# A recurrent layer and a gated feed-forward layer in one kernel: input projection by half blocks, two chains from the first state, VectorE pieces of one width, and five weight pieces rounded by GpSimd

## The chip, the cores and the metric

The kernel runs on 1 core of one Trainium2 chip. The time is device microseconds (us). Before the change the median of 3 runs is 580.43 us (580.22 to 582.93). The execution that the profile shows took 580.79 us, with a span of 579.0 us between its first and last instruction.

## The reference

For 2 sequences of 1024 tokens of 512 numbers, all in float32:

```python
# layer 1, recurrent
u = einsum('bsd,hd->bsh', layernorm(x), W_in) + b_in        # 512 -> 1024
s_t = tanh(u_t + s_{t-1} * gamma + beta)                     # 1024 steps, elementwise
x = x + layernorm(einsum('bsh,dh->bsd', s, W_out) + b_out)   # 1024 -> 512
# layer 2, feed-forward; q(w) rounds a weight to float8_e4m3fn and back
h = layernorm(x)
gate = silu((h @ q(gate_w)) * gate_scale)                    # 512 -> 1536
up = (h @ q(up_w)) * up_scale
x = x + layernorm(((gate * up) @ q(down_w)) * down_scale)    # 1536 -> 512
```

The recurrence is the only part that cannot be computed side by side: state t needs state t-1. The 36 weight pieces of layer 2 (128x512 each) are rounded once, during the first blocks.

## The kernel before

Time is cut into 8 blocks of 128 tokens, with both sequences in a block (256 rows). The names carry the block: u(n) is the input projection of block n, y(n,b) the output projection of its half b (64 tokens of both sequences), gate_up(p,i) and down(p,i) chunk i of 12 of layer 2 for block p.

The recurrence takes one step per token. A step is a scan on VectorE (preact = u + gamma * state, in PSUM) and a tanh on ScalarE that writes the state into `pairs`. The scan of the next step waits for that tanh. For states 0 to 255 one scan of 128x32 and one tanh carry both sequences (L1169, L1470: one chain). From state 256 on each sequence has a scan of 128x16 and a tanh of its own (L1160, L1466: two chains), and the second has the PSUM bank `recur_second`, which up to then served the rounding of weights.

All other work is laid between the steps by a planner. `Timetable.lay` goes through time in tenths of a step and gives each engine the able job of lowest rank; on VectorE and ScalarE a job takes one place between two steps. `timetable` states the jobs, what each waits for and its rank, with costs in steps (`U_STEPS` and the like, times `PACE`). TensorE's jobs run in the order in which they are stated; the table `BETWEEN` says before which chunk of block p a y, u or transpose stands ("y1" is y(p+1,1)). The planner gives places only. On the chip each engine runs its instructions in that order and waits at semaphores.

VectorE's work of a block comes in pieces: adding b_out to y (L1208), statistics (L1174), normalizing (L1227, L1263), the low part of x1 (L1279), scaling z (L1310), and the product of gate and up (L1297, "fused"). `row_parts` cuts most rows of blocks 2 to 7 into four pieces of 128 columns, where the first two blocks have two of 256; `chunk_parts` cuts the gate-up product of blocks 1 to 6 into two of 128 tokens.

A weight piece is rounded by adding and subtracting a constant per number (two VectorE instructions make the constant, L1345 and L1352). 24 pieces do it by three TensorE products into a PSUM bank and two ScalarE copies out of it (L1111 to L1113, L1517); 12 by two accumulating DMAs that GpSimd issues (L1603, L1614).

## Time and profile before

| | us |
|---|---|
| median of 3 runs | 580.43 |
| profiled execution, time | 580.79 |
| profiled execution, span | 579.0 |
| TensorE busy | 553.5 (96%) |
| VectorE busy | 447.2 (77%) |
| ScalarE busy | 371.6 (64%) |
| GpSimd busy | 204.5 (35%) |

The columns of a timeline row are the start, the duration, the engine, the line of the kernel and the shapes; at the end, in brackets, is the idle time of that engine just before and what ended it. Instructions of one engine overlap: the next one starts before the last has ended, so the distance between two starts is what an instruction costs its engine.

### The profile page before, as it was taken

What the parts mean: (1) busy time and instruction counts of PE and PEld (TensorE: products, weight loads), DVE (VectorE), ACT (ScalarE), POOL (GpSimd) and SP (SyncE); (2) the same over time, 40 slices, a digit from 0 to 9 for tenths busy, and PEclk for the clock granted to TensorE, in tenths of its full rate; (3) what the DMA queues carried; (4) which work ended last, traced back from release to release, by engine and by line L of the source; (5) the groups of instructions that cost most, each with busy time, mean ns of one, the idle gap of its engine ahead of it and who ended that gap; (6) DMA issues with size and microseconds to landing.
All of it is one profiled execution on the core that took longest, in us unless ns stands there. A gap on an engine that the chain in (4) does not pass through costs nothing.

```text
span 579.0 us, 11854 instructions
## 1 busy us (share of the span) xinstructions
PE 553.5 (96%) x2984; PEld 462.6 (80%) x2984; DVE 447.2 (77%) x2607; ACT 371.6 (64%) x2284; POOL 204.5 (35%) x339
## 2 busy tenths in 40 slices
PE   8999899899988999999999999999999999999993
PEld 5767667889776988788988799778986897889992
DVE  3689899996796888888988887789868988754313
ACT  3687687855686767866777677767776776523330
POOL 1214316435252323533334333152214341732622
PEclk9999999999998999999999999999999999999997
DMA  7878369800102001010102010020000200200000
GB/s 253 285 225 244 60 201 208 170 0 2 38 1 74 1 2 38 31 45 1 38 2 73 2 38 1 1 74 2 2 1 2 73 2 2 72 1 2 1 36 37
DMA packets 20069, 33.89 MB, mean 59 GB/s; under 512 B 2720, under 2 KB 4896, under 8 KB 20000
## 3 DMA queue, kind: packets, MB, share of 16 engines
q1 hardware_dynamic: 16544, 26.84, 13.8%
q0 software_dynamic: 3456, 6.29, 6.1%
q8 instruction: 24, 0.39, 0.3%
q14 instruction: 45, 0.37, 0.2%
HBM read 22.63 MB, written 4.19 MB: 46 GB/s over the span
## 4 chain that ended last, share of the span: by engine, by line
DVE 50%; ACT 24%; PE 17%; issue 5%; POOL 2%; SPq 0%; DMA 0%; POOLq 0%; DVEq 0%; ACTq 0%
DVE recur L1160 14%; ACT pairs L1466 10%; PE gate_up L1067 8%; DVE recur L1169 6%; DVE recur_second L1160 6%; DVE fused L1297 5%; ACT pairs L1450 4%; PE wide L1090 4%; ACT fused_hi L1509 3%; DVE peaks L1362 3%; ACT gated L1493 3%; PE wide L1026 3%; DVE powers L1345 2%; ACT pairs L1470 2%; DVE rounders L1352 2%
## 5 line engine op out<-in xcount | busy, mean ns | idle before, releaser
L1466 ACT ACTIVATE pairs<-recur 128x8 f32<-128x8 f32 x768 | 138.4, 180 | 100.2 <-DVE recur L1160 99.6
L1160 DVE TENSOR_TENSOR_SCAN recur<-recur,pairs 128x16 f32<-128x16 f32 x768 | 151.3, 197 | 56.0 <-ACT pairs L1466 51.8
L1592 POOL TENSOR_TENSOR fused_lo<-fused,fused_hi 128x256 fp32r<-128x256 f32 x96 | 71.1, 741 | 200.2 <-ACT fused_hi L1509 200.2
L1466 ACT ACTIVATE pairs<-recur_second 128x8 f32<-128x8 f32 x768 | 138.3, 180 | 0.0
L1160 DVE TENSOR_TENSOR_SCAN recur_second<-recur_second,pairs 128x16 f32<-128x16 f32 x768 | 133.4, 174 | 0.0
L1026 PE MATMUL wide<-w_out_sb,pairs 128*128 128x512 f32 x256 | 117.3, 608 | 5.7 <-ACT pairs L1466 5.7
L1067 PE MATMUL gate_up<-x_hi,gate_q 128*128 128x256 f32 x384 | 103.3, 302 | 3.5 <-DVE fused L1297 2.4
L1026 PEld LDWEIGHTS wide<-w_out_sb,pairs 128*128 128x128 f32 x256 | 74.4, 298 | 38.5 <-ACT pairs L1466 7.5
L1004 PE MATMUL wide<-x_norm_t,w_in_sb 128*128 128x256 f32 x448 | 101.0, 380 | 2.3 <-DVE y L1208 2.2
L1004 PEld LDWEIGHTS wide<-x_norm_t,w_in_sb 128*128 128x128 f32 x448 | 84.5, 190 | 16.0 <-issue 3.1
L1067 PE MATMUL gate_up<-x_lo,up_q 128*128 128x256 f32 x384 | 95.9, 283 | 0.0
L1067 PE MATMUL gate_up<-x_hi,up_q 128*128 128x256 f32 x384 | 95.7, 282 | 0.0
L1067 PE MATMUL gate_up<-x_lo,gate_q 128*128 128x256 f32 x384 | 95.2, 281 | 0.0
L1297 DVE SCALAR_TENSOR_TENSOR fused<-gate_up,up_scale_cols,gated 128x128 f32<-128x128 f32 (+1 forms) x168 | 57.9, 349 | 36.2 <-ACT gated L1493 36.2
L1067 PEld LDWEIGHTS gate_up<-x_hi,gate_q 128*128 128x128 f32 x384 | 72.1, 188 | 9.9 <-DVE fused L1297 3.5
L1090 PE MATMUL wide<-down_q,fused_hi 128*128 128x512 f32 x192 | 77.7, 405 | 0.0
L1067 PEld LDWEIGHTS gate_up<-x_lo,gate_q 128*128 128x128 f32 x384 | 72.4, 188 | 5.6 <-issue 3.1
L1090 PE MATMUL wide<-down_q,fused_lo 128*128 128x512 f32 x192 | 75.8, 395 | 0.0
L1067 PEld LDWEIGHTS gate_up<-x_lo,up_q 128*128 128x128 f32 x384 | 72.4, 189 | 0.0
L1067 PEld LDWEIGHTS gate_up<-x_hi,up_q 128*128 128x128 f32 x384 | 72.3, 188 | 0.0
L1169 DVE TENSOR_TENSOR_SCAN recur<-recur,pairs 128x32 f32<-128x32 f32 x256 | 58.9, 230 | 17.0 <-ACT pairs L1470 13.4
L1470 ACT ACTIVATE pairs<-recur 128x16 f32<-128x16 f32 x256 | 48.2, 188 | 36.8 <-DVE recur L1169 34.0
(126 smaller groups left out, 763.8 us busy)
## 6 DMA issues: line engine op xcount, KB each, us to landing
x_in<-x SPq DMA_DIRECT2D x16, 256.0 KB, 3.3
x_res<-x SPq DMA_DIRECT2D x16, 256.0 KB, 3.2
out<-z SPq DMA_DIRECT2D x14, 256.0 KB, 2.5
w_in_sb<-w_in_t SPq DMA_DIRECT2D x4, 512.0 KB, 6.1
w_out_sb<-w_out_t SPq DMA_DIRECT2D x8, 256.0 KB, 4.3
raw_own<-down_w SPq DMA_DIRECT2D x8, 256.0 KB, 3.8
raw_own<-rounders POOLq DMA_DIRECT2D x6, 256.0 KB, 4.5
raw_own<-gate_w SPq DMA_DIRECT2D x5, 256.0 KB, 4.1
```

The source lines that it names most:

```text
L1004: ins = eng.matmul(wide[bank][:, jj * TOK:(jj + 1) * TOK], w_in_sb[:, k, j * P:(j + 1) * P], x_norm_t[:, k, :], start=(k == 0), stop=(k == ...
L1026: ins = eng.matmul(wide[b][:, :], pairs_by_batch[:, state_slots(n, b), :, j, 0].rearrange("p s b -> p (s b)"), w_out_sb[:, j, :], start=(j ...
L1067: ins = eng.matmul(gate_up[g][:, v, :], w_q[:, k, i * P:(i + 1) * P], part[:, k, :], start=(k == 0 and part is x1_hi), stop=(k == KD - 1 a ...
L1090: ins = eng.matmul(wide[2 + b][:, :], part[:, f, b * P:(b + 1) * P], down_q[:, i, :], start=(i == 0 and part is fused_hi), stop=(i == KI - ...
L1160: eng.tensor_tensor_scan(preact_of[b].rearrange("p c k -> p (c k)"), factors_of[b].rearrange("p c k -> p (c k)"), pairs[:, (t - 1) % RING, ...
L1169: eng.tensor_tensor_scan(preact.rearrange("p c k -> p (c k)"), factors.rearrange("p c k -> p (c k)"), pairs[:, (t - 1) % RING, :, :].rearr ...
L1297: eng.scalar_tensor_tensor(out=fused[:, f, ts], in0=gate_up[i % NG][:, 1, ts], scalar=up_scale_cols[:, i:i + 1], in1=gated[:, f, ts], op0= ...
L1362: eng.tensor_reduce(peaks[:, i, h:h + 1], pieces[i][1][:, halves(h)].bitcast(F32), AX_X, ALU.max, apply_absolute_value=True).then_inc(s_pe ...
L1450: ins = eng.activation(pairs_by_batch[:, slots, :, j, 1].rearrange("p s b -> p (s b)"), wide[m % 2][:, at_bank:at_bank + count * batch], A ...
L1466: eng.activation(pairs[:, t % RING, columns, 0], preact_of[b][:, :, 1], ACT.Tanh).then_inc(s_state_of[b], 1)
L1470: eng.activation(pairs[:, t % RING, :, 0], preact[:, :, 1], ACT.Tanh).then_inc(s_state, 1)
L1592: eng.tensor_tensor(fused_lo[:, f, :], fused[:, f, :], fused_hi[:, f, :].bitcast(F32), ALU.subtract).then_inc(s_fused_lo, 1)
```

## The change

- Both chains run from the first state, each sequence with a PSUM bank of its own (`recur0`, `recur1`). `recur_second` goes; the tensor rounding alternates between two banks instead of three.
- All row pieces are halves of 256 columns, and a gate-up product is one piece of 256 tokens in every block.
- The input projection is made by half blocks: 128 columns of one half instead of 256 of both, 16 products an item as against 8. A half can be projected and copied without the other. Block 2's first half is laid ahead of state 128.
- Weight pieces 7, 11, 15, 19 and 23 are rounded on GpSimd by an add and a subtract of 128x512 ("lift", "drop"). 19 pieces stay on TensorE and ScalarE, 12 on DMAs.
- The planner's tables move with it; looking for the weights' peaks starts at step 120 instead of 60. In TensorE's order the last y, y(7,1), stands two chunks later.

```diff
 BETWEEN = {
...
-    6: {4: "y1", 12: "t0 t1"},
+    6: {1: "y02", 2: "y03", 6: "y1", 12: "t0 t1"},
 }
-PEAKS_FROM = 60.0
+PEAKS_FROM = 120.0
+POOL_PIECES = (7, 11, 15, 19, 23)
+ADD_STEPS, LIFT_RANK = 2.7, 0.0
-TWO_CHAINS_FROM = 2
-def row_parts(kind, n, b, last):
-    if kind == "x":
-        return 4 if n >= TWO_CHAINS_FROM + 2 else 2
-    if kind in ("z", "low"):
-        return 2
-    return 2 if n < 2 or (n, b) == (last, 1) else 4
-def chunk_parts(p, last):
-    return 2 if 1 <= p < last else 1
...
-        recur = ps("recur", [P, 2, CH, 2])
-        preact = recur[:, 0, :, :]
-        factors = recur[:, 1, :, :]
+        recur = [ps(f"recur{b}", [P, 2, KH, 2]) for b in range(batch)]
+        preact = [recur[b][:, 0, :, :] for b in range(batch)]
+        factors = [recur[b][:, 1, :, :] for b in range(batch)]
-        recur_second = ps("recur_second", [P, 512])
-        round_banks = [recur_second[:, :], wide[2][:, :], wide[3][:, :]]
+        round_banks = [wide[2 + b][:, :] for b in range(batch)]
...
             def project_u():
-                        for jj in range(2):
-                            j = 2 * m + jj
+                        for jj in range(4):
+                            j = 4 * bank + jj
                             for k in range(KD):
-                                ins = eng.matmul(wide[bank][:, jj * TOK:(jj + 1) * TOK],
-                                                 w_in_sb[:, k, j * P:(j + 1) * P], x_norm_t[:, k, :],
+                                ins = eng.matmul(wide[bank][:, jj * P:(jj + 1) * P],
+                                                 w_in_sb[:, k, j * P:(j + 1) * P], x_norm_t[:, k, g * P:(g + 1) * P],
                                                  start=(k == 0), stop=(k == KD - 1))
...
             def recurrence():
-                    if t >= SPLIT:
-                        for b in range(batch):
...
-                    eng.tensor_tensor_scan(preact.rearrange("p c k -> p (c k)"), factors.rearrange("p c k -> p (c k)"),
-                                           pairs[:, (t - 1) % RING, :, :].rearrange("p c k -> p (c k)"), 0.0,
-                                           ALU.mult, ALU.add).then_inc(s_preact, 1)
+                    for b in range(batch):
+                        if t == 0:
+                            eng.wait_ge(s_bias, 1 + batch)
+                        else:
+                            eng.wait_ge(s_state[b], t)
+                        eng.tensor_tensor_scan(preact[b].rearrange("p c k -> p (c k)"),
+                                               factors[b].rearrange("p c k -> p (c k)"),
+                                               pairs[:, (t - 1) % RING, b * KH:(b + 1) * KH, :].rearrange(
+                                                   "p c k -> p (c k)"), 0.0, ALU.mult, ALU.add).then_inc(s_preact[b], 1)
...
             def fuse():
-                        for h in token_pieces(p):
-                            ts = token_slice(p, h)
-                            eng.scalar_tensor_tensor(out=fused[:, f, ts], in0=gate_up[i % NG][:, 1, ts],
-                                                     scalar=up_scale_cols[:, i:i + 1], in1=gated[:, f, ts],
-                                                     op0=ALU.mult, op1=ALU.mult).then_inc(s_fused, 1)
+                        eng.scalar_tensor_tensor(out=fused[:, f, :], in0=gate_up[i % NG][:, 1, :],
+                                                 scalar=up_scale_cols[:, i:i + 1], in1=gated[:, f, :],
+                                                 op0=ALU.mult, op1=ALU.mult).then_inc(s_fused, 1)
...
+            def round_pieces():
+                for i in range(NP):
+                    if not by_pool(i):
+                        continue
+                    yield at["lift", i]
+                    eng.wait_ge(s_raw_in[raw_of[i]], 16 * (raw_use[i] + 1))
+                    eng.wait_ge(s_constant, i + 1)
+                    eng.tensor_tensor(raw[raw_of[i]], raw[raw_of[i]], rounders[rounder_of[i]].bitcast(F32),
+                                      ALU.add).then_inc(s_lifted, 1)
+                    yield at["drop", i]
+                    eng.wait_ge(s_lifted, pool_pieces(i + 1))
+                    eng.tensor_tensor(pieces[i][1], raw[raw_of[i]], rounders[rounder_of[i]].bitcast(F32),
+                                      ALU.subtract).then_inc(s_dropped, 1)
```

What stands on VectorE between the scans of steps 0 to 1023, counted over the instructions in order (1023 places, at most one instruction in each):

| between two steps | before | after |
|---|---|---|
| nothing | 313 | 497 |
| an aggregate or another of a few columns | 61 | 59 |
| a piece of 128 columns | 240 | 0 |
| a piece of 256 columns | 200 | 320 |
| a gate-up product of 128 tokens | 126 | 0 |
| a gate-up product of 256 tokens | 12 | 76 |
| 128x512, for a weight's constant | 71 | 71 |

In TensorE's order, 61.5 us of work stand between the starts of y(6,1) and y(7,1) after the change, 57.7 us before, and 483.8 us ahead of y(7,1), 484.7 us before (the counts of products times the durations that the trace shows for their kinds).

VectorE in block 3, where y(3,0) is taken up. Before (an instruction named `recur` or `recur_second` is a scan):

```order
L1160 SCALAR_TENSOR_TENSOR recur_second<-recur_second,pairs 128x16
L1208 TENSOR_TENSOR y<-wide,b_out_rows 128x128
L1160 SCALAR_TENSOR_TENSOR recur<-recur,pairs 128x16
L1160 SCALAR_TENSOR_TENSOR recur_second<-recur_second,pairs 128x16
L1208 TENSOR_TENSOR y<-wide,b_out_rows 128x128
L1160 SCALAR_TENSOR_TENSOR recur<-recur,pairs 128x16
L1160 SCALAR_TENSOR_TENSOR recur_second<-recur_second,pairs 128x16
L1208 TENSOR_TENSOR y<-wide,b_out_rows 128x128
```

After the change:

```order
L1234 SCALAR_TENSOR_TENSOR fused<-gate_up,up_scale_cols,gated 128x256
L1110 SCALAR_TENSOR_TENSOR recur<-recur,pairs 128x16 x2
L1151 TENSOR_TENSOR y<-wide,b_out_rows 128x256
L1110 SCALAR_TENSOR_TENSOR recur<-recur,pairs 128x16 x2
L1151 TENSOR_TENSOR y<-wide,b_out_rows 128x256
L1110 SCALAR_TENSOR_TENSOR recur<-recur,pairs 128x16 x2
```

Four places with a piece of 128 columns have become two with 256, and the gate-up product ahead of them is one of 256.

TensorE around the first output projection (`w_out_sb`), in the time of rounding. Before:

```order
L1004 MATMUL wide<-x_norm_t,w_in_sb 128x256 x8
L1026 MATMUL wide<-w_out_sb,pairs 128x512 x8
L1004 MATMUL wide<-x_norm_t,w_in_sb 128x256 x16
L1111 MATMUL wide<-x_norm,ident 128x512
L1112 MATMUL wide<-x_lo,fused_hi 128x512
```

After the change:

```order
L1072 MATMUL wide<-rounders,fused_hi 128x512
L1073 MATMUL wide<-rounders,fused_hi 128x512
L986 MATMUL wide<-w_out_sb,pairs 128x512 x8
L1071 MATMUL wide<-x_res,ident 128x512
L1072 MATMUL wide<-rounders,fused_hi 128x512
L1073 MATMUL wide<-rounders,fused_hi 128x512
L961 MATMUL wide<-x_norm_t,w_in_sb 128x128 x32
```

The input projections are twice as many products of half the columns, and half of block 1's stand ahead of the y.

GpSimd in the same time, after the change (`L1558` is the lift, `L1562` the drop; the DMA rows are issues for the other pieces):

```order
L1558 TENSOR_TENSOR x_res<-x_res,rounders 128x512
L1548 DMA up_q<-z 128x512
L1481 TENSOR_SCALAR norms<-mean_var_y 128x1
L1484 TENSOR_TENSOR norms<-norms,minus_half 128x1
L1548 DMA up_q<-x_norm 128x512
L1512 TENSOR_TENSOR x_res<-y,x_res 128x512
L1562 TENSOR_TENSOR up_q<-x_res,rounders 128x512
L1558 TENSOR_TENSOR raw_own<-raw_own,rounders 128x512
```

The roots of the norms (`norms`) and the residual add (`L1512`), which VectorE waits for, now stand among lifts and drops.

## Rows read from the trace of the kernel before

**Rows 1.** The page: the busy time of each engine.

```profile
PE 553.5 (96%) x2984; PEld 462.6 (80%) x2984; DVE 447.2 (77%) x2607; ACT 371.6 (64%) x2284; POOL 204.5 (35%) x339
```

**Rows 2.** Timeline of TensorE: first and last of four y that waited for a state.

```profile
175.30 5.04 PE L1026 MATMUL wide<-w_out_sb,pairs 128*128 128x512 f32 x7 [3.87 <-ACT pairs L1466]
...
442.89 1.63 PE L1026 MATMUL wide<-w_out_sb,pairs 128*128 128x512 f32 x3 [0.81 <-ACT pairs L1466]
```

**Rows 3.** Timeline of VectorE: the first and the last scan.

```profile
17.75 0.23 DVE L1169 TENSOR_TENSOR_SCAN recur<-recur,pairs 128x32 f32<-128x32 f32 x1 [3.37 <-ACT pairs L1431]
...
501.15 0.20 DVE L1160 TENSOR_TENSOR_SCAN recur<-recur,pairs 128x16 f32<-128x16 f32 x1
```

**Rows 4.** The chain of waits after the last state: start, duration, what.

```profile
501.77 7.18 PE wide L1026 x16
508.95 1.91 PE gate_up L1067 x16
510.86 0.93 PE wide L1090 x4
...
568.84 0.76 DVE z L1310 x2
```

**Rows 5.** Timeline of VectorE, two chains: steps with nothing between.

```profile
300.33 0.20 DVE L1160 TENSOR_TENSOR_SCAN recur<-recur,pairs 128x16 f32<-128x16 f32 x1 [0.16 <-ACT pairs L1466]
...
300.78 0.20 DVE L1160 TENSOR_TENSOR_SCAN recur<-recur,pairs 128x16 f32<-128x16 f32 x1 [0.16 <-ACT pairs L1466]
```

**Rows 6.** The same, a step with a piece of 128 columns.

```profile
313.42 0.20 DVE L1160 TENSOR_TENSOR_SCAN recur<-recur,pairs 128x16 f32<-128x16 f32 x1
...
313.62 0.27 DVE L1208 TENSOR_TENSOR y<-wide,b_out_rows 128x128 f32<-128x128 f32 x1
313.87 0.20 DVE L1160 TENSOR_TENSOR_SCAN recur<-recur,pairs 128x16 f32<-128x16 f32 x1
```

**Rows 7.** The same, a step with a piece of 256 columns.

```profile
302.25 0.18 DVE L1160 TENSOR_TENSOR_SCAN recur<-recur,pairs 128x16 f32<-128x16 f32 x1
...
302.43 0.41 DVE L1310 TENSOR_TENSOR z<-wide,down_scale_rows 128x256 f32<-128x256 f32 x1
302.75 0.18 DVE L1160 TENSOR_TENSOR_SCAN recur<-recur,pairs 128x16 f32<-128x16 f32 x1
```

**Rows 8.** The same, the one step with a gate-up product of 256 tokens.

```profile
146.48 0.20 DVE L1160 TENSOR_TENSOR_SCAN recur<-recur,pairs 128x16 f32<-128x16 f32 x1 [0.22 <-ACT pairs L1466]
...
146.67 0.46 DVE L1297 SCALAR_TENSOR_TENSOR fused<-gate_up,up_scale_cols,gated 128x256 f32<-128x256 f32 x1
147.05 0.19 DVE L1160 TENSOR_TENSOR_SCAN recur<-recur,pairs 128x16 f32<-128x16 f32 x1
```

**Rows 9.** Timeline of VectorE, one chain: a step with an instruction of 128x512.

```profile
89.05 0.23 DVE L1169 TENSOR_TENSOR_SCAN recur<-recur,pairs 128x32 f32<-128x32 f32 x1
89.19 0.41 DVE L1345 TENSOR_SCALAR powers<-raw_own 128x512 int32<-128x512 int32 x1
89.53 0.23 DVE L1169 TENSOR_TENSOR_SCAN recur<-recur,pairs 128x32 f32<-128x32 f32 x1
```

**Rows 10.** The chain of waits: input projections of 128 and of 256 columns.

```profile
9.49 7.16 PE wide L968 x64
...
61.05 7.14 PE wide L1004 x32
```

**Rows 11.** Timeline of TensorE: the starts of two rounded pieces.

```profile
21.37 1.02 PE L1111 MATMUL wide<-raw_own,ident 128*128 128x512 f32 x2
...
22.69 1.02 PE L1111 MATMUL wide<-raw_own,ident 128*128 128x512 f32 x2
```

**Rows 12.** GpSimd's adds of 128x512, and one instruction each of GpSimd and VectorE.

```profile
L1578 POOL TENSOR_TENSOR x_res<-y,x_res 128x512 f32<-128x512 f32 x15 | 19.5, 1303 | 9.7 <-DVE y L1227 9.7
...
134.67 0.78 POOL L1560 TENSOR_SCALAR x_in<-x_in,norms 128x512 f32<-128x512 f32 x1
...
134.81 0.78 DVE L1263 TENSOR_SCALAR x_norm<-x_res,mean_var_r,norms 128x256 f32<-128x256 f32 x1
```

More of the change, by code:

```diff
@@ L128, in lay @@
                 steps = job.steps
-                if engine not in ("vector", "scalar") and self.two_chains_from <= now < self.last_step:
+                if engine not in ("vector", "scalar") and 0 <= now < self.last_step:
                     steps *= PACE
@@ L245, in project_u @@
     def project_u(n, m, k):
-            after = [((*("t1_copy", n, b), h), 0.2) for b in range(batch) for h in range(2)]
+            g = m // 2
+            after = [(v, 0.2) for v in pair("t1_copy", n, g)]
             if m >= 2:
@@ L444, in lay_first @@
             if i == 2:
-                after += converted(i for i in range(NP) if not by_transfer(i))
+                after += converted(i for i in range(NP) if by_tensor(i))
             if i == FIRST_Y_AT_CHUNK:
@@ L490, in timetable @@
                 if i < KI:
-                    low = [(v, 0.2) for b in range(batch) for v in rows("low", "x1_low", p, b)] if i == 0 else []
+                    low = [(v, 0.2) for b in range(batch) for v in pair("x1_low", p, b)] if i == 0 else []
                     gate_up(p, i, low, rank(n - 1, 4.5) + 0.01 * i)
@@ L508, in timetable @@
         norm_z(LAST, b, ("down", LAST, KI - 1), rank(NB, 10 + b))
-    last_piece = max(i for i in range(NP) if not by_transfer(i))
-    for h in range(2):
-        side("vector", ("second", h), [(v, 0.2) for v in pair("take", last_piece)], 90.0)
     t.jobs["down", 0, KI - 1].after.append((("guard", 3), 0.2))
```

379 lines of the change are left out of this document (170 added, 209 removed), and 10 rows, old and new, of the table BETWEEN.

## The prediction, made before the changed kernel ran

> **What bounds the kernel now.** I read the page's busy times first, then TensorE's timeline for its waits, then the chain of waits behind the last state, then VectorE's timeline step by step. TensorE is busy for 553.5 us, 96% of the span [rows 1], which looks like the bound. But its timeline shows output projections that waited for a state: y(2,0) for 3.87 us and, the last of four, y(6,1) for 0.81 us [rows 2]. The last scan starts at 501.15 [rows 3] and y(7,1) at 501.77 [rows 4]: TensorE gets there as its state gets ready. Behind it the chain is TensorE alone up to 568.84, and then the norm and store of the last rows until the span's end at 579.0 [rows 4]. So the end is the start of y(7,1) plus what is left for TensorE (67.1 us) plus 10.2 us, and that start is the later of two things: the recurrence (1023 steps in 483.4 us, 0.473 each [rows 3]) and TensorE's own work ahead of it.
>
> What a step costs is set by VectorE. With two chains a step with nothing between takes 0.45 us, from scan to scan [rows 5]; there VectorE idles and the tanh is waited for. A piece of 128 columns fits into that idle time: 0.45 [rows 6]. A piece of 256 columns doesn't: 0.50 [rows 7]. A gate-up product of 256 tokens makes it 0.57 [rows 8]. With one chain a step with an instruction of 128x512 takes 0.48 [rows 9].
>
> **The change part by part.** *Wider pieces.* Quarters become halves in blocks 2 to 7 and two gate-up products become one. By the counts of the 1023 places between steps: 1023 x 0.45 = 460.4; 320 pieces of 256 columns at 0.05 more, 16.0; 76 wide gate-up products at 0.12 more, 9.1; 71 instructions of 128x512. The trace has none of these last between two chains. From below they cost as a piece of 256 columns (0.05), since their 0.41 us is that piece's [rows 7, 9]; from above as a gate-up product (0.12). I take 0.07, near the first: 5.0. Pieces of a few columns cost nothing. Together 490.5.
>
> The same prices for the kernel before (200 pieces of 256, 12 wide products, 71 at 0.05) give 460.4 + 10.0 + 1.4 + 3.6 = 475.4, where 483.4 were measured [rows 3]. The other 8.0 are waits, two input copies in one step, and the first 255 steps, which had one chain. I carry them over.
>
> *Two chains from the first state.* In the first 255 steps one chain cost 0.48 with a wide instruction between [rows 9], two chains cost 0.50, so about 200 filled places lose 0.02 each, 4.0, and about 50 empty ones gain up to 0.03, 1.5. The bounds of the sum are -1.5 (the filled ones lose nothing) and +4.0 (the empty ones gain nothing); I take 1.5, between them, since both kinds are in the order.
>
> The recurrence then ends at 17.75 + 490.5 + 8.0 + 1.5 = 517.8, against 501.15, and y(7,1) can start 0.6 later, as before: 518.4.
>
> *TensorE.* Five rounded pieces go. One costs 1.32 us, from start to start [rows 11]: 6.6 us less. The half-block input projections double the instructions, but 64 of 128 columns take 7.16 us and 32 of 256 take 7.14 [rows 10], so they cost 0. With two rounding banks instead of three a rounding product can wait for a copy two pieces back; that falls into the time ahead of y(2,0), where TensorE had 3.87 us to wait [rows 2], and I take 0. Ahead of y(7,1) are 483.8 us of work, 0.9 less than before, because that y stands two chunks later (2 x (1.91 + 0.93) = 5.7 [rows 4]). With the idle time of before (501.77 - 484.7 = 17.1) TensorE would be there at 500.9. It won't be: y(6,1) waits for state 896, and from there 61.5 us of TensorE's work stand against 128 steps of about 0.48, also 61.5. So TensorE and state arrive together again, near 518, and I take the state's 518.4; if TensorE is behind, by 1 to 2 us.
>
> *Behind y(7,1)* are 67.1 - 5.7 = 61.4 us [rows 4]. The six chunks behind the last y give 17 us for its norms (6 x 2.84); before there were eight, 22.7.
>
> *Lifts and drops.* Ten adds of 128x512 on GpSimd, 1.30 us each by the nearest row [rows 12]: 13 us on an engine that is busy 35% of the time [rows 1]. They take 10 of ScalarE's copies away, which lay between steps and cost nothing. What they can cost is VectorE's time: while GpSimd worked on 134.67 to 135.45, a VectorE instruction of 256 columns ran for 0.78 [rows 12], where such a piece else takes 0.41 [rows 7], with the next scan queued behind it. The least is 0, the most 10 x 1.30 = 13 us. I take 0, because the 15 such adds of before [rows 12] can have cost only a part of the 8.0 us that all waits made; the range keeps the rest. DMA issues that queue behind a lift on GpSimd come up to 1.3 us later, for weights that are used far later. Of this the Trainium skill (SBUF — State Buffer, Who interferes with whom) says that the two engines share a port pair as an exclusive lock, and whichever comes second blocks for the whole instruction. The row agrees with it, 0.78 against 0.41 us; taken at its worst for all ten, it gives the 13 us of the second rival.
>
> *Sum.* 518.4 + 61.4 + 10.2 = 590.0 of span; with the 1.8 us around it (580.79 - 579.0) 591.8; the median of the runs was 0.4 below the profiled time, so 591.5, which is 1.9% slower.
>
> **Rivals.** *The wider pieces relieve the recurrence: faster.* VectorE would save instructions (240 quarters and 126 halves become 120 and 64), the steps would run at the empty step's pace, and TensorE's saving would come out: y(7,1) at 500.9, the end at 500.9 + 61.4 + 10.2 + 1.8 = 574.3. It decides if steps average below 0.46. For it: 366 short instructions become 184. Against it: the short pieces cost nothing in their steps [rows 6], so there is nothing to save, and the wide ones stand out [rows 7, 8]. The Trainium skill (VectorE: DVE Perf Modes, The TRN2 errata) would have it this way: a fixed latency per instruction, so that few wide tiles beat many small ones. The steps of this trace don't bear it out: 0.57 for a wide product, 0.45 for a step that holds a short piece.
>
> *The lifts collide: slower still.* If six of the ten hold up a VectorE instruction for 1.3 us each, and the scan behind it, the end is some 8 us later: 600. For it: the lock in rows 12, and that 71 instructions of weights stand in the same stretch. Against it: the planner keeps such pairs apart, and few collided before.
>
> *The saving makes up for it: no change.* If only half of the added 17 us comes, because steps with an empty place behind a wide one catch up, the recurrence ends at 509 and the end is near 583; at 507 it is the time of before. The rows speak against it: after a wide step the next one is not shorter than 0.45 [rows 5, 6].
>
> **How the numbers follow.** Forecast 0.77 (its own range 587 to 597), collision 0.10, faster 0.06, no change 0.07. The predicted time is the forecast's, 591.5. The range 585 to 600 takes in the uncertain terms: 4 us below for carried waits that may shrink, 3 below for the 128x512 and one-chain terms; 8 above for collisions and a late TensorE. A measurement tells about 0.5% (2.9 us) from no change. Faster 0.06; within 0.5% 0.06 (the case of no change but for its slower end); slower 0.88.
>
> **What would show it.** Right: the last scan starts near 518, steps with a 256-column piece take 0.50 and with a product 0.57; y(2,1) to y(7,1) mostly wait for a state, longer than before; from y(7,1)'s start to the last product 61 us; TensorE's busy time near 547. Wrong: the last scan before 510 (the prices of wide pieces fail), VectorE instructions of weights that last over 0.8 us beside a lift (collision), a gap on TensorE ahead of the last x1 transposes (the 17 us were too few), TensorE late at y(2,0) for want of a rounding bank, or input products of 128 columns at more than 0.115 us each.

## The result, and the profile after

The changed kernel takes 594.66 us (median of 4 runs, 593.08 to 596.07), the kernel before 580.35 (4 runs beside them). The ratio of their means is 1.0235, with a 95% interval of 1.0196 to 1.0274. By the medians it is slower by 14.3 us. The forecast was 591.5 us in a range of 585 to 600. The profiled execution of the changed kernel took 594.35 us, its span 592.6.

First the page of the changed kernel, the busy time of each engine.

```profile
PE 554.9 (94%) x3412; PEld 477.5 (81%) x3412; DVE 434.6 (73%) x2664; ACT 379.4 (64%) x2530; POOL 218.5 (37%) x349
```

Against [rows 1], VectorE has 12.6 us less to do and GpSimd 14.0 more. TensorE, which gave five rounded pieces away, is not less busy but 1.4 us more: 554.9, where the prediction had 547.

The timeline of VectorE in the changed kernel, the first and the last scan (start, duration, what):

```profile
18.06 0.28 DVE L1110 TENSOR_TENSOR_SCAN recur<-recur,pairs 128x16 f32<-128x16 f32 x2 [4.06 <-ACT pairs L1369]
...
517.19 0.28 DVE L1110 TENSOR_TENSOR_SCAN recur<-recur,pairs 128x16 f32<-128x16 f32 x2 [0.16 <-ACT pairs L1403]
```

The chain of waits of the changed kernel from the last state on, and further down in it the first row of z:

```profile
518.48 1.90 PE gate_up L1027 x16
521.31 6.87 PE wide L986 x16
528.18 1.91 PE gate_up L1027 x16
...
579.11 3.27 PE wide L1050 x14
...
582.40 0.76 DVE z L1246 x2
```

Against [rows 3] the last scan is 16.0 us later (517.19 for 501.15). Against [rows 4], y(7,1) starts 19.5 us later, and from there to z are 61.1 us instead of 67.1. So the 13.6 us that the span grew are 16.0 of recurrence, plus 3.5 because TensorE came to y(7,1) later than the state (521.31 - 517.19 is 4.1 us, before it was 0.6), minus 6.0 behind it.

The 16.0 us of recurrence can be split at step 256, ahead of which no piece on VectorE became wider. The scan of that step on VectorE's timeline, in the kernel before and in the changed one:

```profile
145.48 0.20 DVE L1160 TENSOR_TENSOR_SCAN recur<-recur,pairs 128x16 f32<-128x16 f32 x1 [0.47 <-ACT pairs L1470]
```

```profile
151.71 0.27 DVE L1110 TENSOR_TENSOR_SCAN recur<-recur,pairs 128x16 f32<-128x16 f32 x2
```

From the first scan to this one took 127.7 us before and 133.7 after, 5.9 more; from this one to the last 355.7 and 365.5, 9.8 more; 0.3 lie ahead of the first scan.

The steps of the changed kernel, on VectorE's timeline with two chains: empty ones and, at 301.48, one with a wide gate-up product.

```profile
300.08 0.28 DVE L1110 TENSOR_TENSOR_SCAN recur<-recur,pairs 128x16 f32<-128x16 f32 x2 [0.17 <-ACT pairs L1403]
300.53 0.28 DVE L1110 TENSOR_TENSOR_SCAN recur<-recur,pairs 128x16 f32<-128x16 f32 x2 [0.17 <-ACT pairs L1403]
300.97 0.28 DVE L1110 TENSOR_TENSOR_SCAN recur<-recur,pairs 128x16 f32<-128x16 f32 x2 [0.16 <-ACT pairs L1403]
301.48 0.28 DVE L1110 TENSOR_TENSOR_SCAN recur<-recur,pairs 128x16 f32<-128x16 f32 x2 [0.23 <-ACT pairs L1403]
301.67 0.46 DVE L1234 SCALAR_TENSOR_TENSOR fused<-gate_up,up_scale_cols,gated 128x256 f32<-128x256 f32 x1
302.05 0.27 DVE L1110 TENSOR_TENSOR_SCAN recur<-recur,pairs 128x16 f32<-128x16 f32 x2
```

0.45 and 0.44 empty (the third empty one took 0.51), 0.57 with the product (301.48 to 302.05): the prices of [rows 5] and [rows 8] hold here. Over all steps from state 256 on, the changed kernel has 449 empty ones of 0.456 us on average, 206 with a piece of 256 columns of 0.498 and 67 with a wide product of 0.569. In the kernel before, 240 steps with a piece of 128 columns took 0.461 and 126 with a product of 128 tokens 0.445. What the prediction priced at 0 lies in the first two blocks. VectorE's and then GpSimd's timeline there:

```profile
74.33 0.28 DVE L1110 TENSOR_TENSOR_SCAN recur<-recur,pairs 128x16 f32<-128x16 f32 x2
74.51 1.98 DVE L1281 TENSOR_SCALAR powers<-z 128x512 int32<-128x512 int32 x1
76.41 0.27 DVE L1110 TENSOR_TENSOR_SCAN recur<-recur,pairs 128x16 f32<-128x16 f32 x2
```

```profile
74.00 0.89 POOL L1537 DMA_DIRECT2D z<-rounders  x1 [2.55 <-DVE rounders L1288]
74.65 1.54 POOL L1562 TENSOR_TENSOR up_q<-raw_own,rounders 128x512 fp32r<-128x512 f32 x1
```

An instruction of weights that takes 0.41 us by itself [rows 9] lasted 1.98 beside a DMA issue and a drop, and ended 0.3 us behind the drop; the step took 2.08 us. The 71 steps with an instruction of 128x512 average 0.619 in the changed kernel, with a median of 0.52: 7.1 us over the median, nearly all of it in eight steps, five of them beside a lift or a drop (5.1 us). In three of these five the lift or drop had begun first, as here, on VectorE's and then GpSimd's timeline:

```profile
80.79 1.23 DVE L1281 TENSOR_SCALAR powers<-raw_own 128x512 int32<-128x512 int32 x1
```

```profile
80.16 1.56 POOL L1562 TENSOR_TENSOR up_q<-x_res,x_lo 128x512 fp32r<-128x512 f32 x1
```

VectorE's instruction ended at 82.02, again 0.3 us behind the drop. And TensorE waits in this stretch. Its timeline, four of the waits:

```profile
60.74 9.01 PE L961 MATMUL wide<-x_norm_t,w_in_sb 128*128 128x128 f32 x64 [2.43 <-DVE y L1151]
...
77.06 1.12 PE L1071 MATMUL wide<-z,ident 128*128 128x512 f32 x2 [2.19 <-DVE x_lo L1288]
...
106.85 0.63 PE L1005 MATMUL wide<-ident,x_norm 128*128 128x128 f32 x4 [2.01 <-ACT down_q L1451]
...
114.84 0.39 PE L1027 MATMUL gate_up<-x_hi,gate_q 128*128 128x256 f32 x1 [3.35 <-DVE x_lo L1219]
```

The first 150 us in one row each (length, then busy time of PE, PEld, DVE, ACT, POOL, granted clock, DMA), of the kernel before and of the changed kernel:

```profile
0.00:150.00 150.00, 142.01 (x679) 108.67 (x680) 121.00 (x513) 99.84 (x455) 51.23 (x84) 1.00 0.59 159
```

```profile
0.00:150.00 150.00, 132.45 (x737) 105.10 (x738) 125.42 (x730) 103.31 (x668) 58.67 (x82) 0.97 0.60 159
```

TensorE was idle for 8.0 us before and for 17.6 after. Up to the start of y(7,1) it was busy for 486.0 us before and 493.4 after, and idle for 15.8 and 27.9. So two things in the result were open. The total came out 3 us from the forecast although the lifts did collide and TensorE was late: did the terms cancel? And what made TensorE late, when its work should have shrunk?

### The profile page after: what moved, and what is told of

The parts are those of the page before. It is cut to its first block, busy times and chain, and to the rows that moved or that the text cites. A ratio compares the mean times of both kernels' runs of the same rounds, so it can differ in the third digit from the quotient of the medians.

```text
span 592.6 us, 13054 instructions
## 1 busy us (share of the span) xinstructions
PE 554.9 (94%) x3412; PEld 477.5 (81%) x3412; DVE 434.6 (73%) x2664; ACT 379.4 (64%) x2530; POOL 218.5 (37%) x349
## 3 DMA queue, kind: packets, MB, share of 16 engines
q1 hardware_dynamic: 16544, 26.84, 13.6%
q0 software_dynamic: 3456, 6.29, 6.1%
## 4 chain that ended last, share of the span: by engine, by line
DVE 41%; ACT 29%; PE 24%; issue 4%; DMA 1%; POOL 1%; SPq 0%; POOLq 0%; DVEq 0%; ACTq 0%
DVE recur L1110 21%; ACT pairs L1403 14%; PE gate_up L1027 11%; ACT pairs L1389 6%; PE wide L1050 5%; PE wide L986 5%; DVE fused L1234 4%; ACT gated L1427 3%; DVE peaks L1298 3%; ACT fused_hi L1443 2%; PE wide L961 2%; DVE powers L1281 2%; DVE y L1151 1%; DVE x_norm L1204 1%; DVE x_lo L1219 1%
## 5 line engine op out<-in xcount | busy, mean ns | idle before, releaser
L1403 ACT ACTIVATE pairs<-recur 128x8 f32<-128x8 f32 x2048 | 264.3, 180 | 144.6 <-DVE recur L1110 144.1
L1110 DVE TENSOR_TENSOR_SCAN recur<-recur,pairs 128x16 f32<-128x16 f32 x2048 | 280.8, 183 | 98.5 <-ACT pairs L1403 89.7
L1027 PE MATMUL gate_up<-x_hi,gate_q 128*128 128x256 f32 x384 | 105.3, 307 | 11.0 <-DVE x_lo L1219 9.1
L961 PEld LDWEIGHTS wide<-x_norm_t,w_in_sb 128*128 128x128 f32 x896 | 106.4, 196 | 7.9 <-ACT x_norm_t L1356 3.5
L961 PE MATMUL wide<-x_norm_t,w_in_sb 128*128 128x128 f32 x896 | 107.6, 280 | 4.5 <-DVE y L1151 2.4
L1234 DVE SCALAR_TENSOR_TENSOR fused<-gate_up,up_scale_cols,gated 128x256 f32<-128x256 f32 x96 | 44.6, 464 | 33.4 <-ACT gated L1427 33.2
L1427 ACT ACTIVATE gated<-gate_up,gate_scale_cols 128x256 f32<-128x256 f32 x96 | 45.2, 470 | 32.6 <-PE gate_up L1027 32.6
L1389 ACT ACTIVATE pairs<-wide,u_bias 128x128 f32<-128x128 f32 (+2 forms) x136 | 54.2, 446 | 1.6 <-PE wide L961 1.6
L1443 ACT CAST fused_hi<-fused 128x256 fp32r<-128x256 f32 x96 | 38.4, 400 | 10.8 <-DVE fused L1234 10.5
L1050 PEld LDWEIGHTS wide<-down_q,fused_lo 128*128 128x128 f32 x192 | 36.1, 188 | 5.2 <-issue 0.5
```

The source lines that it names most:

```text
L961: ins = eng.matmul(wide[bank][:, jj * P:(jj + 1) * P], w_in_sb[:, k, j * P:(j + 1) * P], x_norm_t[:, k, g * P:(g + 1) * P], start=(k == 0) ...
L1027: ins = eng.matmul(gate_up[g][:, v, :], w_q[:, k, i * P:(i + 1) * P], part[:, k, :], start=(k == 0 and part is x1_hi), stop=(k == KD - 1 a ...
L1050: ins = eng.matmul(wide[2 + b][:, :], part[:, f, b * P:(b + 1) * P], down_q[:, i, :], start=(i == 0 and part is fused_hi), stop=(i == KI - ...
L1110: eng.tensor_tensor_scan(preact[b].rearrange("p c k -> p (c k)"), factors[b].rearrange("p c k -> p (c k)"), pairs[:, (t - 1) % RING, b * K ...
L1234: eng.scalar_tensor_tensor(out=fused[:, f, :], in0=gate_up[i % NG][:, 1, :], scalar=up_scale_cols[:, i:i + 1], in1=gated[:, f, :], op0=ALU ...
L1389: ins = eng.activation(pairs_by_batch[:, slots, :, j, 1].rearrange("p s b -> p (s b)"), wide[bank][:, at_bank:at_bank + count * batch], AC ...
```

## The experiments

The theory: the recurrence sets the end, and its length is the width of VectorE's pieces. The rivals: it is the lifts; or it is TensorE. I undid parts in the changed kernel, and made parts alone in the kernel before. The ratio compares each with the kernel before on the same chip (there 580.5 to 582.3 us). The time is the median of 4 to 12 executions; the last scan and y(7,1) are read from one profiled execution, which can be off that median by 2.5 us: it took 597.2 us with wide pieces and 601.0 with y(7,1) earlier, the longest of four each, and 595.88 without lifts, the shortest of four.

| kernel | last scan | y(7,1) starts | time, us | ratio to before, interval |
|---|---|---|---|---|
| before | 501.15 | 501.77 | 580.35 | |
| changed | 517.19 | 521.31 | 594.66 | 1.0235 (1.0196 to 1.0274) |
| before, wide pieces | 517.56 | 518.15 | 594.71 | 1.023 (1.02 to 1.026) |
| changed, narrow pieces | 509.02 | 515.28 | 588.22 | 1.0111 (1.0086 to 1.0136) |
| changed, no lifts | 512.37 | 522.83 | 597.77 | 1.0268 (1.024 to 1.0295) |
| changed, both undone | 505.48 | 517.62 | 590.98 | 1.0152 (1.0135 to 1.0169) |
| before, lifts | 515.06 | 515.68 | 594.85 | 1.0235 (1.0212 to 1.0257) |
| before, y(7,1) later | 502.29 | 508.60 | 582.41 | 1.0007 (0.9992 to 1.0022) |
| before, lifts and y(7,1) later | 515.24 | 521.57 | 595.42 | 1.0246 (1.0221 to 1.0272) |
| before, two chains from the start | 503.87 | 507.22 | 586.48 | 1.0087 (1.0062 to 1.0111) |
| before, two rounding banks | 500.80 | 501.45 | 581.80 | 1.0015 (0.9998 to 1.0031) |
| before, split input products | 502.70 | 503.35 | 583.86 | 1.0037 (1.0023 to 1.005) |
| changed, y(7,1) earlier | 519.67 | 520.26 | 598.59 | 1.0307 (1.0281 to 1.0334) |
| before, z and low in quarters | 498.10 | 507.80 | 586.57 | 1.0096 (1.0079 to 1.0113) |

**The wide pieces alone, on the kernel before.**

```
 def row_parts(kind, n, b, last):
-    if kind == "x":
-        return 4 if n >= TWO_CHAINS_FROM + 2 else 2
 ...
+    return 2
 def chunk_parts(p, last):
-    return 2 if 1 <= p < last else 1
+    return 1
```

> The kernel before with VectorE's side work in wide pieces only (halves of 256 columns for every y, x, residual and z, the gate-up product over 256 tokens at once); two chains, input products, rounding and order as before. Theory A (the price of a recurrence step follows the width of the piece that stands in it): 120 more steps with a 256-column piece at 0.05 us and 64 more with the wide product at 0.12 us, 13.7 us, so the last scan near 515 us instead of 501.15 and a time of 591 to 595 us. Rival B (the later end comes from GpSimd's lifts and drops and from the new order, not from width): last scan within 3 us of 501, time 578 to 583 us. Rival C (wide pieces relieve VectorE, fewer instructions): last scan before 501, time under 579 us.

Last scan 517.56, time 594.71: theory A, and the two rivals that deny the width are out, on this kernel. The last scan moved by 16.4 us, for 13.7 expected; but the profiled execution was 2.5 us longer than the median. There are long steps in the trace, which no price of a piece explains. One of them, on VectorE's timeline:

```profile
503.05 0.20 DVE L1156 TENSOR_TENSOR_SCAN recur<-recur,pairs 128x16 f32<-128x16 f32 x1 [0.16 <-ACT pairs L1462]
...
505.15 0.42 DVE L1306 TENSOR_TENSOR z<-wide,down_scale_rows 128x256 f32<-128x256 f32 x1 [1.81 <-PE wide L1086]
505.49 0.19 DVE L1156 TENSOR_TENSOR_SCAN recur<-recur,pairs 128x16 f32<-128x16 f32 x1
```

The step took 2.44 us: a piece of z stands in VectorE's order ahead of the next scan and waits for TensorE, which the longer recurrence has put behind its plan. From state 256 on four steps took 1.5 to 2.4 us each, three of them with a piece of y or z that waited so; the fourth (1.82) stands in the kernel before too (1.81). These three are 4.1 us over a usual step, a step ahead of them took 3.25 us where it took 1.56 before, and the first scan came 0.4 us later. That leaves some 10 us for the width.

**The narrow pieces put back into the changed kernel** (quarters, and the gate-up product in two halves, planner and waits with them).

```
+def row_parts(kind, n, b, last):
+    if kind == "x":
+        return 4 if n >= TWO_CHAINS_FROM + 2 else 2
 ...
+def chunk_parts(p, last):
+    return 2 if 1 <= p < last else 1
```

> The changed kernel with the narrow pieces of the kernel before put back (quarters of y, x and residual in the later blocks, the gate-up product in two halves of 128 tokens in blocks 1 to 6); two chains from the start, half-block input products, five pieces on GpSimd and the new order stay. Theory A: the last scan falls by 12 to 14 us, to 503 to 505 us; y(7,1) then starts when TensorE comes to it, between 503 and 510 us, and with 61 us behind it the time is 575 to 583 us. Rival B (lifts, drops and order made the later end): last scan stays at 514 to 517 us, time 590 to 595 us. Rival T (TensorE sets the end, with its dearer input products and its lower clock): last scan earlier, but y(7,1) not before 515 us, time 588 us or more.

8.2 us of the last scan come back, not 12 to 14, and 6 to 7 of the time (588.22 for 594.66; ratio 1.0111 for 1.0235). The last scan on VectorE's timeline, and y(7,1) in the chain of waits:

```profile
509.02 0.28 DVE L1162 TENSOR_TENSOR_SCAN recur<-recur,pairs 128x16 f32<-128x16 f32 x2
```

```profile
515.28 6.87 PE wide L1038 x16
```

The numbers are rival T's: the last scan is earlier, but y(7,1) starts at 515.28, 6 us behind the state, and the time is 588.22. That the width lengthens the recurrence holds as well, all of it behind step 256 (365.5 us from there on with wide pieces, 357.1 with narrow ones). And TensorE's arrival hangs on the width too. Its waits for the low part of x1 (line, engine waited for, us in total, times, longest) from 150 to 515 us, in the changed kernel and then with narrow pieces:

```profile
PE gate_up L1027 <- DVE x_lo L1219: 5.7, 3, 2.5
PE wide L986 <- DVE x_lo L1219: 1.7, 1, 1.7
```

```profile
PE gate_up L1079 <- DVE x_lo L1273: 2.4, 3, 1.1
```

7.4 us became 2.4, which is most of the 6.0 us by which y(7,1) starts earlier (515.28 for 521.31); in the kernel before it was 1.0. VectorE makes x1's low part between its steps, so what makes the steps longer can reach TensorE this way.

**No lifts in the changed kernel.**

```
-POOL_PIECES = (7, 11, 15, 19, 23)
+POOL_PIECES = ()
```

> The changed kernel with no piece of weights rounded by GpSimd (24 pieces on TensorE in the two banks); the rest as changed. In the profile of the changed kernel nine steps of the first two blocks that meet a lift or a drop are 7 us over the median together. Theory A with collisions as a second cause: these steps go back to 0.5 us, last scan at 509 to 512 us instead of 517; TensorE has five pieces of 1.32 us more, 6.6 us, ahead of y(7,1), which then starts at 515 to 522 us; time 588 to 595 us. Rival without collisions (the long steps have another source, transfers of weights or ScalarE): last scan stays at 516 to 518 us, time 594 to 599 us. Rival B (collisions and order are all of it): last scan near 503 us.

The last scan is at 512.37, 4.8 us earlier, as theory A has it but for 0.4 us, and the 71 steps of 128x512 average 0.517 instead of 0.619. The collisions were the lifts'. These steps alone give back 7.2 us; others became longer, one of 2.76 us with a copy of y. But y(7,1) starts at 522.83, 10.5 us behind the state, and the time of 597.77 is above theory A's range: with five pieces more TensorE alone sets the end. The lifts cost the recurrence 4.8 us, and taking them out doesn't make this kernel faster; the intervals of the two ratios overlap.

**Half-block products alone, on the kernel before.** Each product of 256 columns as two of 128.

```
-for jj in range(2):
-    j = 2 * m + jj
+for jj in range(4):
+    j, g = 2 * m + jj // 2, jj % 2
     for k in range(KD):
-        eng.matmul(wide[bank][:, jj * TOK:(jj + 1) * TOK], ..., x_norm_t[:, k, :], ...)
+        eng.matmul(wide[bank][:, jj * P:(jj + 1) * P], ..., x_norm_t[:, k, g * P:(g + 1) * P], ...)
```

> The kernel before with each input product of 256 columns (28 items of 8 products, blocks 1 to 7) done as two products of 128 columns into the same bank; copies, order and the rest unchanged. Theory H (the half-width products cost 0.2 us more per item, as 3.49 us against 3.26 us in the two profiles): 28 items make TensorE 5 to 7 us busier, 559 us instead of 553.5, and since TensorE hardly waits in this kernel the time is 583 to 587 us. Rival K (the 3.49 us are a lower clock in that stretch, or waits inside an item, and the products cost the same per column): TensorE 553 to 555 us busy, time 579.5 to 582 us.

Between the theories, and nearer to H: TensorE is 3.1 us busier (556.6), half of what H said, and the time of 583.86 is in H's range, 0.37% or some 2.2 us over the kernel before beside it. The line of these products, in the kernel before, in this one and in the changed kernel (busy us, mean ns, idle before). Each product of the program leaves two instructions in the trace, so an item of 8 products of 256 columns shows as x16 and one of 16 of 128 as x32.

```profile
L1004 PE MATMUL wide<-x_norm_t,w_in_sb 128*128 128x256 f32 x448 | 101.0, 380 | 2.3 <-DVE y L1208 2.2
```

```profile
L1004 PE MATMUL wide<-x_norm_t,w_in_sb 128*128 128x128 f32 x896 | 104.3, 275 | 2.2 <-DVE y L1208 2.0
```

```profile
L961 PE MATMUL wide<-x_norm_t,w_in_sb 128*128 128x128 f32 x896 | 107.6, 280 | 4.5 <-DVE y L1151 2.4 <-ACT x_norm_t L1356 2.0
```

The split costs this line 3.3 us, half of the 6.6 that rounding saves. In the chain of waits one item shows it: 16 instructions of 256 columns (from the kernel with y(7,1) later, below, which has them whole), and 32 of 128 (from the one with both losses undone):

```profile
284.08 3.45 PE wide L1004 x16
```

```profile
292.13 3.57 PE wide L1013 x32
```

28 items at 0.12 us more are 3.4 us. The changed kernel's line has another 3.3 us. A part of it comes with a lower granted clock: the 64 instructions behind the wait of 2.43 us at 60.74 took 9.01 us, where 64 such take 7.16 [rows 10], and the mean granted clock from 60 to 70 us was 0.83.

**The lifts alone, on the kernel before** (the same five pieces, with `round_pieces` of the changed kernel).

> The kernel before with pieces 7, 11, 15, 19 and 23 rounded by GpSimd (lift and drop) instead of TensorE; narrow pieces, chains, input products and order as before. Theory A (lifts and drops hold up VectorE's instructions of weights, and the scan behind them): TensorE 6.6 us less busy, near 547, but the last scan 3 to 7 us later, 504 to 508 us, and the time 583 to 587 us. Rival S (no collision of weight, and the state sets y(7,1) anyway): last scan 500 to 502, time 579.5 to 581.5 us, the saving idle. Rival N (TensorE alone is the bound): time 573 to 577 us.

The mechanism of theory A, but two to four times its size: the last scan is 13.9 us later and the time 594.85. TensorE is not near 547 us either but busy for 553.0, at a granted clock of 0.973 over the whole run (0.991 in the kernel before). VectorE's and ScalarE's timelines at the longest step:

```profile
68.45 0.23 DVE L1206 TENSOR_TENSOR_SCAN recur<-recur,pairs 128x32 f32<-128x32 f32 x1
68.59 0.41 DVE L1389 TENSOR_SCALAR rounders<-powers 128x512 fp32r<-128x512 f32 x1
74.74 0.23 DVE L1206 TENSOR_TENSOR_SCAN recur<-recur,pairs 128x32 f32<-128x32 f32 x1 [5.74 <-ACT pairs L1507]
```

```profile
74.22 0.48 ACT L1487 ACTIVATE pairs<-wide,u_bias 128x128 f32<-128x128 f32 x1 [5.80 <-PE wide L1041]
74.50 0.21 ACT L1507 ACTIVATE pairs<-recur 128x16 f32<-128x16 f32 x1
```

A step of 6.29 us. Ten other steps with an instruction of weights were over 0.62 us, up to 2.28. By step 85 the recurrence was 7.1 us behind that of the kernel before (67.00 for 59.88). VectorE's copy of y came late with it, and TensorE's input projection waited 7.19 us for it (to 67.69, where [rows 10] has it start at 61.05); ScalarE's copy of that projection stands ahead of a tanh; and the scan waits for the tanh. The profile of the changed kernel has eight such steps and none over 2.08 us, and at step 85 it is 1.6 us behind (61.48): no such chain of waits formed there. Which part of its new order prevents it was not tried.

**y(7,1) two chunks later, alone and with the lifts, on the kernel before.**

```
-    6: {4: "y1", 12: "t0 t1"},
+    6: {6: "y1", 12: "t0 t1"},
```

> The kernel before with the last output projection, y(7,1), two chunks later in TensorE's order (at chunk 6 of block 6 instead of 4), nothing else. Theory A (state and TensorE come together at y(7,1)): the two chunks, 5.7 us, go ahead of it, TensorE comes to it at 506 to 508 us, and the time stays at 579 to 582 us. Rival S (TensorE could have come earlier and the state alone sets it): y(7,1) at 502 to 503, time 574 to 577 us.

> Both of the former together: the kernel before with five pieces rounded by GpSimd and y(7,1) two chunks later. Theory A (TensorE and the recurrence each bound the start of y(7,1), so only lighter TensorE work ahead of it and the later place together pay): TensorE at y(7,1) near 501.8 + 5.7 - 6.6 = 501 us, the state there at 502 to 508 depending on collisions, 61.4 us behind it, time 575 to 582 us. Rival (collisions cost what is saved): last scan 507 us or later, time 581 us or more.

Alone: no change (1.0007), y(7,1) at 508.60, as theory A has it but for 0.6 us: what no longer stands behind y(7,1) stands ahead of it. With the lifts: 595.42, the rival, since the last scan is at 515.24 as with the lifts alone.

**Two chains from the start, and two banks alone, on the kernel before.** The first: `TWO_CHAINS_FROM = 0`, the second chain's bank taken out of `round_banks`, its factors filled at the head. The second leaves the chains:

```
-round_banks = [recur_second[:, :], wide[2][:, :], wide[3][:, :]]
+round_banks = [wide[2][:, :], wide[3][:, :]]
```

> The kernel before with two chains from the first state and therefore two banks for rounding instead of three; narrow pieces, 24 pieces on TensorE, full input products and order as before. Theory A (as forecast for this edit): last scan 1.5 us later (0 to 4), 501 to 505 us, time 580 to 584 us, TensorE's idle time ahead of 150 us within 2 us of the 8 us of before. Rival B (two banks and wide weight instructions between two chains hold TensorE and the weights up early): TensorE idle 4 us or more longer ahead of 150 us, last scan 505 us or later, time 585 us or more.

> The kernel before with two banks for rounding (those of the down products) instead of three; one chain up to state 256 and two behind, 24 pieces on TensorE, order as before. Theory A (as the prediction took it: the bank costs nothing, what two chains from the start cost lies in the chains): time 579.5 to 582 us, TensorE's idle time ahead of 150 us 8 to 10 us as before. Rival B (the missing bank makes rounding products wait for copies, and the weights, x1 and the input products behind them): idle time ahead of 150 us 12 us or more, time 584 to 587 us, as with two chains from the start.

The banks are free (1.0015, the interval holds 1). The chains are not. They cost the recurrence 2.7 us, inside the forecast for that edit and theory A's range, but the time 5.1 (0.87%), since TensorE falls behind: its idle time and the time are rival B's, and not for the banks that B named. The first 150 us with two chains from the start, and with two banks alone:

```profile
0.00:150.00 150.00, 134.40 (x620) 101.22 (x621) 123.66 (x754) 108.70 (x693) 48.72 (x80) 0.98 0.61 159
```

```profile
0.00:150.00 150.00, 140.78 (x673) 107.30 (x674) 120.10 (x505) 98.31 (x447) 51.24 (x83) 0.99 0.60 159
```

15.6 and 9.2 us of TensorE idle; before it was 8.0, in the changed kernel 17.6. ScalarE is 8.9 us busier than before with two chains. The longest wait of TensorE in that stretch, in the kernel with two chains from the start:

```profile
113.17 1.22 PE L1001 MATMUL wide<-x_norm_t,w_in_sb 128*128 128x256 f32 x2 [5.39 <-ACT pairs L1441]
```

It waited for ScalarE's input copies. That the second chain's tanhs made these late is what the busier ScalarE suggests; it was not tried apart.

**Both losses of the recurrence undone in the changed kernel** (narrow pieces and no lifts).

> The changed kernel with two parts undone at once: narrow pieces as before and no piece rounded by GpSimd (24 pieces on TensorE in two banks). What is left of the change: two chains from the start with two banks, half-block input products, the new order. Theory A (the recurrence's losses add: 8.2 us for the width and 4.8 us for the lifts, by undoing one at a time): last scan at 503 to 505 us, as in the kernel before with two chains from the start; TensorE, with 5 pieces of 1.32 us more than with lifts, sets y(7,1), at 513 to 520 us, and the time is 586 to 593 us. Rival B (the two losses lie in one another, the state waits for TensorE): last scan at 507 us or later. Rival C (with both gone the state sets the end again): y(7,1) within 1 us of the last state, time under 580 us.

The last scan is at 505.48, just past theory A's range. Seen from this kernel, the width costs 6.9 us (512.37 - 505.48), the lifts 3.5 (509.02 - 505.48), and both 11.7 (517.19). They nearly add. One early step of 4.24 us in this trace, with a copy of y (2.76 without lifts alone), makes the first two look smaller: from step 256 on, where the widths differ, the wide pieces cost 9.0 us (365.7 for 356.7). The 590.98 are TensorE's, 12.1 us behind the state at y(7,1). Against the kernel without lifts y(7,1) is 5.2 us earlier (517.62 for 522.83): TensorE's waits for the low part of x1 from 150 us on fell from 7.4 to 2.4 us here too.

**y(7,1) earlier in the changed kernel** (chunk 4 instead of 6 of block 6).

> The changed kernel with y(7,1) back at chunk 4 of block 6, two chunks earlier; nothing else. Theory A (state 1024 at 517.8 us sets its start, TensorE was 3.5 us late): y(7,1) starts at 518 to 519 us with 66.8 us behind it instead of 61.1, time 596 to 598 us. Rival T (TensorE's work alone sets the end, the place of y(7,1) doesn't matter): time 593.5 to 595 us.

y(7,1) starts with its state, at 520.26, and the time is 598.59, just over theory A's range. The recurrence was 2.5 us longer in the profiled execution, for steps of the first two blocks; that execution took 601.0 us. The row of y(7,1) on TensorE's timeline, and the stretch behind it:

```profile
520.26 8.91 PE L986 MATMUL wide<-w_out_sb,pairs 128*128 128x512 f32 x16 [2.11 <-ACT pairs L1403]
```

```profile
520.00:530.00 10.00, 9.74 (x25) 5.98 (x26) 3.06 (x10) 0.46 (x3) 2.70 (x4) 0.83 0.01 2
```

After the wait the product took 8.91 us instead of 6.87, at a granted clock of 0.83. In the changed kernel, where TensorE came late and didn't wait, the same product took 6.87.

**A version meant to beat both:** the kernel before with z and the low part of x1 in quarters too.

```
     if kind in ("z", "low"):
-        return 2
+        return 4 if (kind == "z" or n > 0) and n < last else 2
```

> The kernel before with the pieces that were still 256 columns wide beside the recurrence narrowed too: z (copy and statistics) of blocks 0 to 6 and the low part of x1 of blocks 1 to 6 in quarters of 128 columns, about 80 pieces. Theory A (steps pay for width, 80 x 0.05 = 4 us, but TensorE becomes the bound, since of its waits for states only 0.59 and 0.81 us lie late): last scan at 497 to 499 us, y(7,1) at 500 to 501 us, time 577.5 to 580 us. Rival S (the state alone sets the end): time 575.5 to 577.5 us. Rival R (more instructions cost VectorE more than width): last scan 501 us or later, time 580.5 us or more.

The last scan is at 498.10, 3.1 us earlier: the price by width holds this way too. The time is 586.57, slower, which none of the theories had. TensorE's and GpSimd's timelines ahead of y(7,1):

```profile
505.73 0.80 PE L1090 MATMUL wide<-down_q,fused_hi 128*128 128x512 f32 x1 [2.47 <-POOL fused_lo L1592]
```

```profile
502.49 2.50 POOL L1584 TENSOR_TENSOR z<-z,x_res 128x512 f32<-128x512 f32 x2
504.95 2.10 POOL L1592 TENSOR_TENSOR fused_lo<-fused,fused_hi 128x256 fp32r<-128x256 f32 x3
```

With more pieces in VectorE's queue the last statistics of z come so late (GpSimd takes them up at 498.61, before at 493.41) that GpSimd does block 6's z just then, and the low part of a gate-up product, which TensorE needs, stands behind it. Another 2.6 us of TensorE's waits behind 150 us are for normalized rows of VectorE, which cost it none in the kernel before. y(7,1) starts at 507.80, 9.7 us behind the state. None of these versions beats the kernel before.

## Why the prediction was right

*The end is the later of the state's and TensorE's arrival at y(7,1), plus 61 us, plus 10.* Right, and 61.1 us were measured for 61.4. The last scan came at 517.19 for 517.8.

*Wider pieces, 15.1 us (490.5 - 475.4).* Right in kind, too dear in size. 13.7 of it lie behind step 256 (120 pieces at 0.05, 64 products at 0.12); undone in the changed kernel they were 8.4 and 9.0 us there, made alone on the kernel before some 10 without its waits, and 9.8 is what the changed kernel lost there. A piece of 256 columns costs its step 0.04 over an empty one (0.498 against 0.456) and not 0.05. And the steps of before were not all at 0.45: its 275 empty ones behind step 256 average 0.464, waits that the prediction carried over whole among its 8.0 us.

*Two chains from the first state, 1.5 us.* 2.7 us of recurrence, inside the bounds. What the step left out is TensorE: 7.6 us of idle time in the first 150 us.

*Lifts and drops, 0.* This step failed. They cost the recurrence 3.5 to 4.8 us, inside the bound of 13. The rival spoke of a planner that keeps such pairs apart. It does so in its plan, but nothing in the program orders the two engines, and on the chip they met (74.51 and 74.65). As the Trainium skill (SBUF — State Buffer, Who interferes with whom) has it, the one that comes second waits for the whole instruction. Where the drop had begun first, the trace agrees: 1.23 us for an instruction of 0.41, ended 0.3 us behind the drop (80.79 against 80.16). It doesn't settle the two longest: there VectorE's instruction began 0.03 and 0.14 us ahead of GpSimd's add, during a DMA issue, and ended 0.3 us behind the add all the same. (The 13 us that the prediction lays to its second rival are the bound of its own sum; that rival has 8.)

*The sum of these.* 15.1 + 1.5 + 0 was forecast, 16.6: 13.7 behind step 256 and 2.9 ahead of it. Measured are 9.8 behind it, 5.9 ahead of it and 0.3 ahead of the first scan, 16.0. The total was right to 0.6 us by luck: the price of width was too high by about as much as the early steps were too cheap. Of the 5.9, two chains alone make 2.3, and the lifts 2.8 to 4.6 (undone with narrow and with wide pieces); what the order and the half blocks add was not taken apart.

*TensorE, "with the idle time of before TensorE would be there at 500.9".* This step failed too, and the larger part of the miss is here. Ahead of y(7,1) TensorE was to have 0.9 us less work and had 7.4 more (493.4 for 486.0), and its idle time grew by 12.1 (27.9 for 15.8). Of the work, 6.6 us are the line of the input products (107.6 for 101.0), which were taken at 0 by [rows 10]. Half of that is the split itself: the 32 instructions of 256 columns in those rows took 7.14 us behind a wait, and two later items of 16 take 2 x 3.45 = 6.90. One row was read for a group of 28. Of the idle time, 9.6 us lie in the first 150 us, where two chains alone open 7.6; behind that TensorE waits 7.4 us for the low part of x1, before 1.0. Nor did y(6,1) wait for state 896: it started 1.7 us behind that step's scan (457.67 for 456.02), without a wait. At y(7,1) TensorE was late by 3.5 us more than before, for 1 to 2 in the prediction. y(7,1) at 521.31 for a forecast of 518.4 is nearly all of the 3.2 us by which the time lies over the forecast.

*The signs.* Of its signs of being wrong two showed: instructions of weights over 0.8 us beside a lift (five, up to 1.98), and input products at more than 0.115 us each (107.6 / 896 = 0.120; 0.116 with the split alone).

*y(2,1) to y(7,1) mostly wait for a state, longer than before.* Wrong, as the line of the output projections shows:

```profile
L986 PE MATMUL wide<-w_out_sb,pairs 128*128 128x512 f32 x256 | 116.6, 600 | 3.0 <-DVE x_lo L1219 1.7 <-ACT pairs L1403 1.2
```

Of 3.0 us of waits 1.2 are for a state, and they are y(0,1)'s. TensorE waits for the low part of x1 instead, 1.4 to 2.5 us at the head of four later stretches.

The rival *the wider pieces relieve the recurrence* is out by both ways of testing it; with narrower pieces the last scan came earlier each time (509.02 for 517.19, 498.10 for 501.15). The rule of the Trainium skill (VectorE: DVE Perf Modes, The TRN2 errata), few wide tiles before many small ones, holds for VectorE's busy time here (424.5 us with wide pieces alone, 447.2 before) and not for a chain that the tiles stand in.

## What to carry to other kernels

Where two engines bound the same point, undoing one part shows the other bound and not that part's cost; read the arrival of each at the meeting point, not only the time: three kernels here, the changed one and those with wide pieces or lifts alone, took 594.7 to 594.9 us, for three different reasons. A piece beside a dependent chain is free as far as it fits into the chain's own wait, and costs its excess; but more pieces in an in-order queue push back what stands last in it. In an order written down ahead, a late instruction holds up whatever stands behind it, so collisions that had cost a chain 7.1 us came out a second time three queues on, as a step that was 5.8 us too long.

## What was not expected of the hardware

- An instruction of 128x512 on VectorE that takes 0.41 us lasted 1.86 to 2.19 us where a DMA issue of GpSimd (0.86 to 1.06 us) was followed by its add of 1.5 us: twice in the changed kernel, twice with the lifts alone.
- The same data in 896 instructions of 128 columns instead of 448 of 256 cost TensorE 3.3 us more (104.3 for 101.0), 0.12 us for each item of 32.
- After waits of 2.1 to 2.4 us the granted clock was 0.83 in the 10 us that followed (60 to 70 us in the changed kernel, 520 to 530 with y(7,1) earlier), so TensorE spent a part of them at the lower of its two levels, and 16 output products took 8.91 us instead of 6.87. Not every such wait did this. Behind this one, on TensorE's timeline of the kernel before, the granted clock was 1.00 from 61 to 71 us:

```profile
61.05 7.14 PE L1004 MATMUL wide<-x_norm_t,w_in_sb 128*128 128x256 f32 x32 [2.16 <-DVE y L1208]
```
